# Null scores beside the values' products, and a loop's first loads issued one stage earlier, in a two-layer transformer kernel

## The reference, cut to what matters

```python
q = (xn @ Wq) per head; k, v = split(xn @ Wkv)          # xn: layer norm of x
nk, nv = null_kv                                        # a key and a value for every query
sim  = concat(q @ nk * scale + null_bias, q @ k.T * scale + bias)   # masked, causal
attn = softmax(sim); out = attn @ concat(nv, v)
```

## Time and profile before

| | |
|---|---|
| median of 3 runs | 3217.09 us (3211.94 to 3220.69) |
| profiled execution, span | 3218.2 us |
| TensorE busy | 2924.2 us (91%) |
| VectorE busy | 1882.8 us (59%) |
| ScalarE busy | 1578.7 us (49%) |
| GpSimd busy | 382.5 us (12%) |
| DMA | 308.23 MB, mean 96 GB/s |

### The profile page before, as it was taken

One profiled execution on the slowest core, in us unless ns is written; L12 is line 12 of the kernel. 1 busy time (PEld: TensorE's weight loads), 2 busy tenths in 40 slices (PEclk: granted clock), 3 DMA queues, 4 the chain that ended last, 5 costly groups with the idle time before them and its releaser, 6 DMA issues. The chain is left out here.

```text
span 3218.2 us, 50056 instructions
## 1 busy us (share of the span) xinstructions
PE 2924.2 (91%) x17179; PEld 2052.1 (64%) x17181; DVE 1882.8 (59%) x4554; ACT 1578.7 (49%) x3849; POOL 382.5 (12%) x729
## 2 busy tenths in 40 slices
PE   7978999899999998758799999998999999959996
PEld 5746666546777777344577777764667777836664
DVE  5456555346777766777577777345667777332223
ACT  4403555426666661644466666233566666213331
POOL 4560000001111100000000000000111111012222
PEclk8998999999999999879899999998999999979998
DMA  4452221245444321005432321006544443341112
GB/s 123 121 171 64 44 55 28 76 158 162 124 146 145 121 88 39 1 20 160 130 86 68 86 68 35 20 10 195 171 138 126 150 125 104 118 159 34 34 35 92
DMA packets 242482, 308.23 MB, mean 96 GB/s; under 512 B 27261, under 2 KB 185085, under 8 KB 242096
## 3 DMA queue, kind: packets, MB, share of 16 engines
q1 hardware_dynamic: 235082, 285.50, 29.1%
q0 software_dynamic: 7152, 19.54, 2.1%
HBM read 231.31 MB, written 73.21 MB: 95 GB/s over the span
## 5 line engine op out<-in xcount | busy, mean ns | idle before, releaser
L2407 ACT ACTIVATE cond_p<-cond_p,cond_negm 128x128 f32<-128x128 f32 (+7 forms) x768 | 593.2, 775 | 408.4 <-DVE cond_negm L2438 407.5
L2388 PE MATMUL ps_o<-cond_pt,cond_v 128*64 128x256 f32 (+1 forms) x3840 | 478.2, 370 | 5.1 <-DVE attn_out L2474 0.5
L2368 PE MATMUL ps_s<-cond_k_high,cond_q_high 128*128 128x512 f32 (+5 forms) x1152 | 439.4, 387 | 16.8 <-DVE cond_negm L2438 8.3
L2438 DVE CUSTOM_DVE_ANT_0 cond_p<-ps_s,cond_side,cond_null_scores 128x128 f32<-128x128 f32 (+7 forms) x512 | 403.7, 811 | 28.1 <-PE ps_s L2369 22.6
L2369 PE MATMUL ps_s<-cond_k_both,cond_q_both 128*128 128x512 f32 (+5 forms) x1152 | 394.1, 344 | 0.0
L2378 PE MATMUL ps_t<-ident,cond_p 128*128 128x128 f32 x2304 | 348.8, 281 | 6.8 <-ACT cond_pt L2412 4.8
L2388 PEld LDWEIGHTS ps_o<-cond_pt,cond_v 128*64 128x64 f32 x3840 | 237.4, 136 | 180.4 <-issue 89.8
L2378 PEld LDWEIGHTS ps_t<-ident,cond_p 128*128 128x128 f32 x2304 | 250.0, 140 | 106.0 <-issue 77.1
L1507 ACT ACTIVATE attn_pt<-ps_t 128x512 f32<-128x512 f32 (+3 forms) x384 | 173.0, 490 | 237.9 <-PE ps_t L1468 174.6
L2368 PEld LDWEIGHTS ps_s<-cond_k_high,cond_q_high 128*128 128x128 f32 x1152 | 219.9, 191 | 40.1 <-DVE cond_negm L2438 22.3
L2446 DVE COPY cond_pt<-ps_t 128x512 f32<-128x512 f32 (+1 forms) x240 | 140.4, 585 | 166.3 <-PE ps_t L2378 164.6
(11 more groups left out here) (503 smaller groups left out, 4682.1 us busy)
## 6 DMA issues: line engine op xcount, KB each, us to landing
mqa_q_halves<-cond_q_cut SPq DMA_DIRECT2D x96, 512.0 KB, 4.7
cond_q_both<-mqa_q_halves SPq DMA_DIRECT2D x384, 128.0 KB, 3.2
cond_q_high<-mqa_q_halves SPq DMA_DIRECT2D x192, 128.0 KB, 3.0
cond_side<-in_fside_16xSxS SPq DMA_DIRECT2D x32, 512.0 KB, 7.2
moe_experts<-in_L_ffn_W SPq DMA_DIRECT2D x16, 1024.0 KB, 12.2
cond_side<-in_fside_16xSxS SPq DMA_DIRECT2D x32, 448.0 KB, 5.6
cond_side<-in_fside_16xSxS SPq DMA_DIRECT2D x32, 384.0 KB, 5.0
cond_side<-in_fside_16xSxS SPq DMA_DIRECT2D x32, 320.0 KB, 4.6
```

What stands on the lines that cost most here:

```text
L2368: nc.tensor.matmul(out, c32(a.Q1[i][:, h, s * P:(s + 1) * P]), c32(a.K1[:, keys]), start=True, stop=False)
L2388: last = nc.tensor.matmul(sums[u % ON][h * HD:(h + 1) * HD, s0 * P:2 * P], a.V[:, b * QB + kb, :], PT[c % PT_SLOTS][:, (2 * h + s0) * P:(h ...
L2407: nc.scalar.activation(p, p, ACT.Exp, bias=negm[u % SMALL][:, r:r + 1], scale=-1.0, accum_out=rsum[u % SMALL][:, r:r + 1]).then_inc(exped, 1)
L2438: nc.vector.tensor_tensor_reduce(out=probs(u, r, 0, q + 1), in0=m.S[k % 2][:, row_offset(L):row_offset(L) + L], in1=toep_back(u, h, L) if ...
```

## The change

In the plain stages the weights of values and null scores stand side by side in one tile `VN` (64 + 16 columns), so one product of a token tile gives both, token-major. These 16 products are no longer a phase of their own: each stands behind one of the jobs 2 to 17. DVE makes the null weights at the block's start, and takes a tile's value and null scores with two instructions. The head-major null scores, their turning and the copy to `SA` go.

In the cosine stage the null scores are made token-major too, two tiles behind each of the tiles 8 to 15, straight in the bank from which DVE reads them. ScalarE's copies and the turning go. `W0`'s sum and the mask row move from tile 0 to tile 5, and the two instructions on `SA` stand ahead of the last low half. SP issues the first four units' query loads behind the stores of tile 10, and the first two `load_toep` behind those of tiles 14 and 15. The null bias is loaded once as a row for all partitions.

```diff
 def stage_mqa_queries(nc, m, d, name, q):
-      for t in range(NT):
+
+      def values_and_nulls(t):
+        if t == 0:
+          pe.wait_ge(weighed, 2)
         if t >= 2:
           pe.wait_ge(v_taken, t - 1)
         for c in range(DC):
-          last = nc.tensor.matmul(m.O[t % 2][:, 0:HD], m.XT[:, c, t * P:(t + 1) * P], wkv[:, c, HD:2 * HD],
+          last = nc.tensor.matmul(m.O[t % 2][:, 0:HD + HEADS], m.XT[:, c, t * P:(t + 1) * P], VN[:, c, :],
                       start=(c == 0), stop=(c == DC - 1))
         last.then_inc(valued, 1)
-      pe.wait_ge(v_taken, NT)
-
-      def null_scores(g):
-        if g == 0:
-          pe.wait_ge(nulled, NULL_READY)
-        else:
-          pe.wait_ge(null_taken, g)
-        for c in range(DC):
-          last = nc.tensor.matmul(m.T[0][0:HEADS, :], W0[:, c, :], m.XT[:, c, g * GRP:(g + 1) * GRP],
-                      start=(c == 0), stop=(c == DC - 1))
-        last.then_inc(null_made, 1)
       for j in range(JOBS):
         project(j)
-        if j in (8, 12, 16, 20):
-          null_scores((j - 8) // 4)
-      pe.wait_ge(null_taken, NG)
-      for t in range(NT):
-        last = nc.tensor.matmul(null_bank[:, t, :], null_t[:, t * P:(t + 1) * P], m.ident[0:HEADS, 0:HEADS],
-                    start=True, stop=True)
-      last.then_inc(null_turned, 1)
+        if VALUES_AT <= j < VALUES_AT + NT:
+          values_and_nulls(j - VALUES_AT)
...
+      nc.vector.tensor_scalar(nk[:, :], nk[:, :], HD ** -0.5, None, ALU.mult).then_inc(nulled, 1)
+      dve.wait_ge(nulled, 1)
+      nc.vector.tensor_tensor(wn[:, :, :], wq_all[:, :, :].rearrange("p c (h w) -> p (c h) w", w=HD),
+                  nk[:, :].unsqueeze(1).broadcast_to([P, DC * HEADS, HD]), ALU.mult).then_inc(nulled, 1)
+      nc.vector.tensor_copy(VN[:, :, 0:HD], wkv[:, :, HD:2 * HD]).then_inc(weighed, 1)
+      dve.wait_ge(nulled, 2)
+      nc.vector.tensor_reduce(VN[:, :, HD:HD + HEADS], wn[:, :, :].rearrange("p (c h) w -> p c h w", c=DC),
+                  mybir.AxisListType.X, ALU.add).then_inc(weighed, 1)
...
-      for t in range(NT):
+      def take_values_and_nulls(t):
         dve.wait_ge(valued, t + 1)
-        nc.vector.tensor_tensor(V[:, t, :], m.O[t % 2][:, 0:HD], nv_row[:, :], ALU.subtract).then_inc(v_taken, 1)
-      nc.vector.tensor_scalar(nk[:, :], nk[:, :], HD ** -0.5, None, ALU.mult).then_inc(nulled, 1)
-      dve.wait_ge(nulled, NULLED)
-      nc.vector.tensor_tensor(wn[:, :, :], wq_all[:, :, :].rearrange("p c (h w) -> p (c h) w", w=HD),
-                  nk[:, :].unsqueeze(1).broadcast_to([P, DC * HEADS, HD]), ALU.mult).then_inc(nulled, 1)
-      dve.wait_ge(nulled, NULLED + 1)
-      nc.vector.tensor_reduce(W0[:, :, :].rearrange("p c h -> p (c h)"), wn[:, :, :], mybir.AxisListType.X,
-                  ALU.add).then_inc(nulled, 1)
+        nc.vector.tensor_tensor(V[:, t, :], m.O[t % 2][:, 0:HD], nv_row[:, :], ALU.subtract)
+        nc.vector.scalar_tensor_tensor(SA[:, t, :], m.O[t % 2][:, HD:HD + HEADS], -1.0, nb_row[:, :],
+                       ALU.mult, ALU.subtract).then_inc(v_taken, 1)
...
-      def take_null(g):
-        dve.wait_ge(null_made, g + 1)
-        piece = null_t[:, g * GRP:(g + 1) * GRP]
-        nc.vector.tensor_scalar(piece, m.T[0][0:HEADS, :], NB[:, 0:1], -1.0, ALU.add, ALU.mult).then_inc(null_taken, 1)
...
       for j in range(JOBS):
         cut_low(j, m.SH[j % 4])
-        if j in (8, 12, 16, 20):
-          take_null((j - 8) // 4)
+        if VALUES_AT <= j < VALUES_AT + NT:
+          take_values_and_nulls(j - VALUES_AT)
         if j == 24:
           cut_keys((k_taken, NG))
-      dve.wait_ge(null_turned, 1)
-      nc.vector.tensor_copy(SA[:, :, :], null_bank)
 def stage_mqa_cosine(nc, m, d, name, q):
...
-  KEYS_AT, NULLS_AT = 3, 8
...
-      sp.dma_start(nb_row[:, :], q.null_bias.rearrange("(a n) -> a n", a=1).broadcast_to([P, HEADS])).then_inc(nb_loaded, 16)
       for t in range(NT):
         i = t % len(cut)
         sp.wait_ge(lows, t + 1)
         for which in range(2):
           sp.dma_start(d["mqa_q"][which, :, t * P:(t + 1) * P].rearrange("(a p) n -> p a n", p=P),
                 cut[i][:, which, :, :]).then_inc(q.stored[i], 16)
-      for u in range(Q_SLOTS):
-        q.load_queries(sp, u)
+        if t == NT // B + 2:
+          for u in range(Q_SLOTS):
+            q.load_queries(sp, u)
+        free = t - len(cut) + 2
+        if NT - len(cut) <= free < NT - len(cut) + 2:
+          sp.wait_ge(q.stored[free % len(cut)], 32 * (free // len(cut) + 1))
+          q.load_toep(sp, free % len(cut))
...
-      def null_scores(g):
-        if g == 0:
+      def null_scores(t):
+        if t == 0:
           pe.wait_ge(weighed, 1)
           pe.wait_ge(k_kept, NG)
-        else:
-          pe.wait_ge(null_kept, g)
         for c in range(DC):
-          last = nc.tensor.matmul(m.O[0][0:HEADS, :], W0[:, c, :], m.XT[:, c, g * GRP:(g + 1) * GRP],
+          last = nc.tensor.matmul(null_bank[:, t, :], m.XT[:, c, t * P:(t + 1) * P], W0[:, c, :],
                       start=(c == 0), stop=(c == DC - 1))
-        last.then_inc(null_made, 1)
+        if t == NT - 1:
+          last.then_inc(null_made, 1)
       for t in range(NT):
         if t >= 2:
...
           turn_queries(t - 1)
         if KEYS_AT <= t < KEYS_AT + NG:
           turn_keys(t - KEYS_AT)
-        if NULLS_AT <= t < NULLS_AT + NG:
-          null_scores(t - NULLS_AT)
+        if t >= NULLS_AT:
+          null_scores(2 * (t - NULLS_AT))
+          null_scores(2 * (t - NULLS_AT) + 1)
       turn_queries(NT - 1)
-      pe.wait_ge(null_kept, NG)
-      for t in range(NT):
-        last = nc.tensor.matmul(null_bank[:, t, :], null_t[:, t * P:(t + 1) * P], m.ident[0:HEADS, 0:HEADS],
-                    start=True, stop=True)
-      last.then_inc(null_turned, 1)
...
         if KEYS_AT <= t < KEYS_AT + NG:
           if t == KEYS_AT:
-            act.wait_ge(weighed, 1)
+            act.wait_ge(key_gain, 1)
...
-        if NULLS_AT <= t < NULLS_AT + NG:
-          g = t - NULLS_AT
-          act.wait_ge(null_made, g + 1)
-          nc.scalar.copy(null_t[:, g * GRP:(g + 1) * GRP], m.O[0][0:HEADS, :]).then_inc(null_kept, 1)
       cut_high(NT - 1)
...
       for t in range(NT):
         measure(t)
         if t == 0:
-          nc.vector.tensor_scalar(gain[:, 0:1], q.ks[:, 0:1], q.qs[0:HD, 0:1], 8.0, ALU.mult, ALU.mult)
+          nc.vector.tensor_scalar(gain[:, 0:1], q.ks[:, 0:1], q.qs[0:HD, 0:1], 8.0, ALU.mult, ALU.mult).then_inc(key_gain, 1)
+        if t == WEIGH_AT:
           dve.wait_ge(gained, 1)
           nc.vector.tensor_reduce(W0[:, :, :].rearrange("p c h -> p (c h)"), q.wn[:, :, :], AX.X, ALU.add).then_inc(weighed, 1)
           dve.wait_ge(cleared, 1)
...
-      cut_low(NT - 1)
-      dve.wait_ge(null_turned, 1)
+      dve.wait_ge(null_made, 1)
+      dve.wait_ge(inverted, NT)
       nc.vector.tensor_tensor(SA[:, :, :], null_bank, q_inv[:, :, :], ALU.mult).then_inc(null_scaled, 1)
       dve.wait_ge(null_scaled, 1)
-      dve.wait_ge(nb_loaded, 16)
       nc.vector.scalar_tensor_tensor(SA[:, :, :], SA[:, :, :], -1.0, nb_row[:, :].unsqueeze(1).broadcast_to([P, NT, HEADS]),
                      ALU.mult, ALU.subtract)
+      cut_low(NT - 1)
 def stage_mqa(nc, m, d, name, w, cosine):
...
-  NB = m.sb(name + "_null_bias", [HEADS, 8], F32, small + 2816)
+  nb_row = m.sb(name + "_null_bias_row", [P, HEADS], F32, small + 2816)
...
-  null_t = m.sb(name + "_null_t", [HEADS, B * S], F32, loop_at + 26624)
+  VN = m.sb(name + "_w_value_null", [P, DC, HD + HEADS], F32, loop_at + 26624)
...
-    load(NB[:, 0:1], column(w.null_bias))
+    load(nb_row[:, :], row(w.null_bias).broadcast_to([P, HEADS]))
...
+  q.load_toep = load_toep
...
-      if cosine:
-        for i in range(a.n_cuts):
-          sp.wait_ge(a.stored[i], 32 * (NT // a.n_cuts))
-        a.load_toep(sp, 0)
-        a.load_toep(sp, 1)
       for u, (pair, b, q0) in enumerate(MQA_UNITS):
```

More of the change, by code:

```diff
@@ L1677, in stage_mqa_queries @@
 def stage_mqa_queries(nc, m, d, name, q):
-    Q1, K1, KW, K2, V, W0, SA, null_t, nk = q.Q1, q.K1, q.KW, q.K2, q.V, q.W0, q.SA, q.null_t, q.nk
-    cut, wkv, wq_all, wn, nv, nv_row, nv_wide, NB, mask = q.cut, q.wkv, q.wq_all, q.wn, q.nv, q.nv_row, q.nv_wide, q.NB, q.mask
+    Q1, K1, KW, K2, V, VN, SA, nk = q.Q1, q.K1, q.KW, q.K2, q.V, q.VN, q.SA, q.nk
+    cut, wkv, wq_all, wn, nv, nv_row, nv_wide, nb_row, mask = q.cut, q.wkv, q.wq_all, q.wn, q.nv, q.nv_row, q.nv_wide, q.nb_row, q.mask
     stored, loaded, load_queries = q.stored, q.loaded, q.load_queries
     keyed, k_taken, valued, v_taken, cut_k = (m.sem(f"{name}_{s}") for s in ("keyed", "k_taken", "valued", "v_taken", "k_cut"))
-    nulled, null_made, null_taken, null_turned, k_cleared = (m.sem(f"{name}_{s}") for s in (
-        "nulled", "null_made", "null_taken", "null_turned", "k_cleared"))
+    nulled, weighed, k_cleared = (m.sem(f"{name}_{s}") for s in ("nulled", "value_null_weighed", "k_cleared"))
```

(31 more changed lines are left out.)

## The result

The changed kernel takes 3180.8 us in the median of four runs (3179.11 to 3190.17), beside 3218.89 for the kernel before in the same comparison: a ratio of 0.9884, 95% interval 0.9862 to 0.9907. The forecast was 3181.0. The profiled execution is the slowest of the four, span 3188.5 us; the other three have spans of 3177.3 to 3179.8. It was 35.6 us ahead of the kernel before at the second plain loop's start (2246.74 us) and lost 6 of them again, 4.3 at 2429 to 2437 and 2.1 at 2800 to 2822 us, in stages whose lines the change does not touch.

The account below looks back on a forecast made before the run. TensorE was taken to pace the plain stages, a ring across engines the cosine stage, and the DMA queue its end. Plain 20.7 plus cosine 15.6 gave 36.3 us off 3218.2: 3181.9, or 3181.0 as median; range 3172 to 3196.

Parts of the forecast that it names:

- plain sum: Both plain query stages: removed products and null scores, less insertions, plus shorter ends; 20.7 us gained, bounds 12.3 to 22.3.
- cosine tail: End of the cosine query stage: query and distance loads issued earlier let the loop's first DVE row start 15.1 us sooner.
- Insertion: Plain stages: four short 80-column matmuls behind a query job cost 0.55 us, at least 0.50, at most 0.81.
- Rival (1): Switching between long and short matmuls costs 0.81 us per insertion, also in the cosine stage; total 3191 us, chance 0.09.
- Plain tails: Last query job to loop in each plain stage: 2.3 us against 4.5 and 5.74; gains 2.2 and 3.4 us.
- rivals (3): Short matmuls between long ones lower TensorE's clock in the plain stages; up to 3291 us, chance 0.06.
- (4): Stores set the plain stages' pace, so only their tails are won there; total 3196 us, chance 0.03.
- Cosine front: Cosine stage, W0's sum and mask row moved: 3.3 us gained at tile 0, 3.5 lost at tile 5, 1.4 lost to clock.
- the ring: Cosine query stage's cycle per tile: PE transposes, ACT high half, low half, DVE scaling of the next tile; 5.08 us.
- Null scores: Cosine stage: eight insertions of eight 16-column matmuls, 1.0 us each, tiles of 5.5 us; gain 2.1, bounds 0 and 3.
- two distance loads of 0.46 to 1544.9: End of cosine stage: SP issues two distance loads after its last stores, 0.46 us each, ending at 1544.9 in old times.
- Rival (2): Distance rows arrive late behind stores on the same queue, so their wait only moves; 6 us less gain, 3187 us, chance 0.06.

Follow-up runs that it names:

- wide: Changed kernel, but each plain-stage insertion moves 160 columns instead of 80 with the same four weight loads; job with insertion 2.26 us, ratio 0.9895 to the kernel before.
- weigh0: Changed kernel, but the weights' sum and mask row are back at tile 0 of the cosine stage; ratio 0.9883 to the kernel before.
- one_toep: Changed kernel, but the second pair's distance rows are requested at the cosine loop's start, not behind the query stage's last stores; ratio 0.9881 to the kernel before.

## Why the prediction was right, step by step

- **Total.** 36.3 us were forecast; the stages show 24.1 + 0.9 + 11.7 = 36.7. The plain sum (20.7) was 3.4 too low and the cosine tail (15.1) 3.4 too high, and they cancelled. Most mechanisms held, but that the forecast came within 1 us is luck, and that the median came within 0.2 of it all the more so, with runs 11 us apart.
- **Insertion: too dear.** I took 0.55 us with 0.50 as the floor; it is 0.45, so 32 of them cost 14.4 us instead of 17.6, 3.2 less. My floor was the mean of a block (0.124 per matmul) with steps of 0.44 and 0.53 in turn; I had taken it for the pure weight load, and the short step would have been right. The step held that 16 more columns are free (0.44 with 64, 0.45 with 80) and that columns and floor do not add up (wide). That the floor is the load of 128 columns fits and is not separated. The Trainium skill ("TensorE: Matmul & The Clock Gate", LDWEIGHTS) has a load's time grow with its columns, 1 ns for 1.2 of them. The estimate by it is 107 ns for such a load and 0.43 us for an insertion, nearer to the 0.45 seen than my row's 0.50. Rival (1), 0.81, is out.
- **Plain tails.** 2.3 us forecast, 2.18 of wait seen; the gains of 2.2 and 3.4 held within 0.2. No query job took over 1.76 us: rivals (3) and (4) are out.
- **Cosine front.** +3.3, -3.5 and -1.4 came as +3.29, -3.48 and -1.42 (against the ring of 5.08); weigh0 turns them back. I had seen that the move costs 1.6 net. That the clock's part came so near is in part luck, since it was 2.3 and 2.7 in two other traces.
- **Null scores.** A tile is 5.29, not 5.5 us: eight matmuls take 0.81 and not 1.0, the same mistake about the floor. The stretch of the last eight tiles gains 2.8, not 2.1, though one tile takes 6.15, which I had not seen: the cut of the keys is on the ring there, while in the kernel before this tile took 6.32 like its neighbours. A few tenths more in the first and the seventh tile leave the front with 0.9.
- **Cosine tail: too cheap.** 15.1 was forecast (12 to 16), 11.7 came, just below the bound. The step that failed is "two distance loads of 0.46 to 1544.9": behind stores and the first pair they hold SyncE for 4.63 us. The landing that I had "there by 1546.2" was hardly better off: one_toep puts it 9.0 us behind the issue, some 1.5 us ahead of the loop's first DVE row, so taking the issue away uncovers the landing. The forecast's tail, 22.7 - 15.1 = 7.6, came only with both the second pair late and the query loads spread (7.57 and 7.60). Rival (2) was half right: the transfers bound the tail, though DVE's named wait was TensorE.

## What to carry to other kernels

Price a short matmul between long ones at the longer of its columns' time and a floor (0.45 us for four here), and take the floor from a stretch that waits for nothing, not from a block's mean. A load moved ahead to stand behind a stage's stores lands later and can hold its issuing engine longer; count what is in the queue, not only the issue. Where two engines get in each other's way, moving one instruction can only move the wait to another; give it company that doesn't wait. Read a gain of 1 us in a stage against how much the same stage differs between traces of unchanged lines.

## What the hardware showed

- Two distance loads took SyncE 0.92 us at the loop's start of the kernel before (1.84 for four), behind query loads of 128 KB; behind stores of 512 KB they took 3.02 and 4.63. The engines' share alone does not tell the two apart: it was 0.83 in the cheap case as well, in this window of the kernel before.

```profile
1554.00:1556.00 2.00, 1.19 (x4) 0.93 (x4) 0.00 (x0) 1.28 (x1) 0.00 (x0) 0.50 0.83 181
```

- Behind a pause of 3.60 us TensorE was at half clock for most of the projection (5.27 instead of 3.60 us, clock 0.66 in the window); behind one of 1.17 it was not. The tile behind the longer pause took 1.4 us more than the ring in nine traces, 2.3 and 2.7 in one each.
- A DVE step of 16 elements waited 3.1 us for a GpSimd product, while a DVE reduction (1.21 us), a step of one element (0.19) and a subtraction that reads PSUM (0.23) beside such a product kept their times.
- Four matmuls with 80 moving columns between long ones cost 0.45 us, with 160 columns 0.55.
